# First tiles by half products, up behind three runs, and VectorE's order within a step

## The reference, cut to what matters

```python
y    = conv1d(x, weight, groups=4, pad=4) + (c @ c_weight.T)[:, :, None] + bias[None, :, None]
base = y @ base_W.T + base_b                          # 512 -> 512
p    = softmax(y @ router_W.T + router_b)             # 15 routes
w    = sum of the top 8 p, by expert (expert_map)     # 8 experts
h    = y @ A.T                                        # 8 experts x rank 16
out  = x + base + 2 * ((h * w) @ B.T)
```

## Time and profile before

| what | value |
|---|---|
| median of three runs | 184.21 us (184.16 to 184.89) |
| the profiled execution's own time | 184.34 us |
| its span in the trace | 182.5 us |
| TensorE busy | 178.0 us, 98% of the span |
| VectorE busy | 151.0 us, 83% |
| GpSimd busy | 139.7 us, 77% |
| ScalarE busy | 81.6 us, 45% |
| chain that ended last | TensorE 92%, DMA 5%, VectorE 1% |

### The profile page before, as it was taken

The page is one execution under the profiler, slowest core; times in us unless marked ns, Lnnn a source line. Parts: engine busy times, 40 slices in busy tenths (PEclk is TensorE's granted clock), DMA queues, the critical chain, the costliest instruction groups (busy, mean ns, idle before and its releaser), DMA issues.

```text
span 182.5 us, 3929 instructions
## 1 busy us (share of the span) xinstructions
PE 178.0 (98%) x1236; PEld 170.9 (94%) x1236; DVE 151.0 (83%) x510; ACT 81.6 (45%) x247; POOL 139.7 (77%) x138
## 2 busy tenths in 40 slices
PE   7999999999999999999999999999999999999993
PEld 3777999999999999999999999999999999999992
DVE  0597888898898889888888988889898888978673
ACT  3568743354544434454433445444344545422320
POOL 2118999999888898888889888888988888885610
PEclk9999999999999999999999999999999999999999
DMA  6999951767475654637475454756536721233304
GB/s 160 355 347 288 340 190 11 234 193 213 161 231 176 187 169 123 198 131 230 132 232 164 133 166 163 230 178 196 188 101 160 278 83 61 94 115 115 119 0 172
DMA packets 17876, 32.01 MB, mean 175 GB/s; under 512 B 1984, under 2 KB 3136, under 8 KB 17856
## 3 DMA queue, kind: packets, MB, share of 16 engines
q1 hardware_dynamic: 17424, 31.40, 53.7%
q10 hardware_dynamic: 432, 0.36, 0.6%
HBM read 23.36 MB, written 8.39 MB: 174 GB/s over the span
## 4 chain that ended last, share of the span: by engine, by line
PE 92%; DMA 5%; DVE 1%; ACT 0%; SPq 0%; issue 0%; DVEq 0%
PE wide_ps L604 61%; PE wide_ps L646 12%; PE conv_banks L590 11%; DMA wide_sb<-wide_w 3%; PE edge_bank L590 3%; PE conv_banks L604 2%; PE odd_bank L633 2%; DMA x_in<-x_first 2%; PE conv_banks L563 1%; PE conv_banks L561 1%; DVE xr L979 1%; ACT wide_hi L356 0%; SPq L257 0%; PE conv_banks L646 0%; PE edge_bank L633 0%
## 5 line engine op out<-in xcount | busy, mean ns | idle before, releaser
L604 PE MATMUL wide_ps<-wide_hi,y_hi 128*128 128x400 f32 (+1 forms) x248 | 66.1, 326 | 0.3 <-ACT wide_hi L356 0.3
L604 PE MATMUL wide_ps<-wide_hi,y_lo 128*128 128x400 f32 (+1 forms) x248 | 62.6, 312 | 0.0
L604 PE MATMUL wide_ps<-wide_lo,y_hi 128*128 128x400 f32 (+1 forms) x248 | 62.4, 312 | 0.0
L484 POOL TENSOR_TENSOR terms_lo<-terms,terms_hi 128x512 fp32r<-128x512 f32 x28 | 36.3, 1297 | 18.2 <-ACT terms_hi L385 18.2
L604 PEld LDWEIGHTS wide_ps<-wide_hi,y_hi 128*128 128x128 f32 x248 | 44.0, 188 | 2.5 <-ACT wide_hi L356 0.6
L604 PEld LDWEIGHTS wide_ps<-wide_lo,y_hi 128*128 128x128 f32 x248 | 45.9, 188 | 0.0
L604 PEld LDWEIGHTS wide_ps<-wide_hi,y_lo 128*128 128x128 f32 x248 | 45.8, 188 | 0.0
L502 POOL TENSOR_TENSOR y_lo<-y,y_hi 128x512 fp32r<-128x512 f32 x31 | 40.3, 1298 | 5.0 <-ACT y_hi L400 5.0
L479 POOL TENSOR_TENSOR xr<-xr,base_b_sb 128x512 f32<-128x512 f32 x32 | 41.7, 1302 | 0.0
L407 ACT ACTIVATE hw_hi<-odd_bank 128x128 fp32r<-128x128 f32 x31 | 8.6, 278 | 54.3 <-PE odd_bank L633 54.3
L779 DVE TENSOR_TENSOR xr<-wide_ps,xr 128x512 f32<-128x512 f32 x30 | 20.7, 691 | 5.3 <-PE wide_ps L646 4.0
(11 more groups left out here) (90 smaller groups left out, 308.8 us busy)
## 6 DMA issues: line engine op xcount, KB each, us to landing
xr<-x_rows SPq DMA_DIRECT2D x32, 256.0 KB, 3.6
out<-xr SPq DMA_DIRECT2D x31, 256.0 KB, 3.3
terms<-x_units SPq DMA_DIRECT2D x28, 256.0 KB, 2.8
edges<-x_edges SPq DMA_DIRECT2D x14, 256.0 KB, 3.2
wide_sb<-wide_w SPq DMA_DIRECT2D x4, 328.0 KB, 5.0
x_in<-x_first SPq DMA_DIRECT2D x3, 264.0 KB, 5.3
weights_sb<-conv_w SPq DMA_DIRECT2D x2, 192.0 KB, 5.8
x_in<-x_first SPq DMA_DIRECT2D x2, 132.0 KB, 2.8
```

Source lines behind the costliest of these rows:

```text
L484: nc.gpsimd.tensor_tensor(terms_lo[i % 2][:, :, :, :], terms[i][:, :, :, :], terms_hi[i % 2][:, :, :, :].bitcast(F32), ALU.subtract)\
L604: mm = nc.tensor.matmul(sums_of(t, k)[:, b, 0:columns[1] - columns[0]], a[k % 2][:, r, :], w[:, r, columns[0]:columns[1]], start=r == 0 an ...
```

## The change

Tiles 2 and 3 no longer come as plain blocks: they are loaded as pairs of terms, as the later tiles are, and `conv_whole` makes them with float32 products of 256 columns: the odd terms by summed weights, the difference by own weights, and, for tile 2 alone, the edges of both tiles. The differences of these tiles are made by GpSimd (tile 2 and the edges) and VectorE (tile 3). In step 0 a `W_REST` run stands ahead of HIGH of run 2. The loads at the start have a new order and new waits, and `base_b` comes as 128 full rows. The bias of the first four tiles is added by GpSimd after the output sum (`bias_sums`) and no longer before it. SyncE issues the load of the next rows ahead of the store. `up` stands behind three runs from step 2 on (two in step 1, three before). The edges of tiles 4 and 6 are made within steps 2 and 4, ahead of `up`. On VectorE `condition` is cut in two (`condition` and `reach`); from step 6 on a step is: condition, hw_low, choose, best, reach, mark, difference, add_out, weigh, turn. Steps 2 to 5 have orders of their own. ScalarE makes `y_high` right behind `hw_high` (behind the exponentials in steps 2 to 4). The last two steps are as before.

The core of the diff:

```diff
+            def conv_whole(t):
+                i, h = t - FIRST, t % 2
+                pe.wait_ge(y_rows_ready, t - 1)
+                pe.wait_ge(conv_w_in[2 + i], 16)
+                pe.wait_ge(first_terms_in[i], 16)
+                nc.tensor.matmul(conv_ps[:, h, 0, :, :], conv_sb[:, W_SUM[t], :],
+                                 first_terms[i][:, 1, :, :], start=True, stop=True)
+                pe.wait_ge(first_difference[i], 1)
+                mm = nc.tensor.matmul(conv_ps[:, h, 1, :, :], conv_sb[:, W_OWN[t], :],
+                                      first_terms[i][:, 0, :, :], start=True, stop=True)
+                if h == 0:
+                    pe.wait_ge(cond_biased, GROUPS)
+                    pe.wait_ge(first_edge_ready, 1)
+                    mm = nc.tensor.matmul(edge_ps, conv_sb[:, W_QUARTERS[t // 2], :],
+                                          first_edges[:, 0, :, :], start=True, stop=True)
+                mm.then_inc(conv_done, 1)
...
                 y_rest(0)
                 y_rest(1)
+                w_rest(0)
                 high(2)
                 y_rest(2)
-                w_rest(0)
+                w_rest(1)
...
             def second_step():
                 linear(1, 1, runs, (FRONT_BANK,), (W_REST,))
+                conv_whole(3)
                 pe.wait_ge(y_lo_ready, 2)
                 linear(1, 1, runs, (FRONT_BANK,), (Y_REST,)).then_inc(front_done, 1)
-                conv_later(3)
                 turn_hw(0, 0)
-                linear(1, 1, runs[:3], (NEXT_BANK,))
+                linear(1, 1, runs[:2], (NEXT_BANK,))
                 up(0, 0)
-                linear(1, 1, runs[3:], (NEXT_BANK,)).then_inc(linear_done, 1)
+                linear(1, 1, runs[2:], (NEXT_BANK,)).then_inc(linear_done, 1)
+                conv_blocks(START, 0)
...
                     turn_hw(t - 1, k - 1)
-                    linear(t, k, runs[:2], (NEXT_BANK,))
+                    linear(t, k, runs[:3], (NEXT_BANK,))
+                    if t == 2 or t == 4:
+                        conv_edges(t + 2, (k + 2) % GROUPS, p + 1).then_inc(conv_done, 1)
                     up(t - 1, k - 1)
-                    linear(t, k, runs[2:], (NEXT_BANK,)).then_inc(linear_done, 1)
+                    linear(t, k, runs[3:], (NEXT_BANK,)).then_inc(linear_done, 1)
...
+                if up_to_tile(t, 5):
+                    if t == 5:
+                        turn(t + 1, k + 1)
+                    hw_low(t - 1, k - 1)
+                    choose(t, k)
+                    dve.wait_ge(logits_ready, t + 1)
+                    best(t, k)
+                    if t < 5:
+                        turn(t + 1, k + 1)
+                    else:
+                        condition(t + 2, (k + 2) % GROUPS, q + (k + 2) // GROUPS)
+                        reach(t + 2, (k + 2) % GROUPS)
+                    dve.wait_ge(top_ready, t + 1)
+                    mark(t, k)
+                    difference(t + 4, k)
+                    add_out(t - 1, (k - 1) % UNROLL)
+                    weigh(t, k)
...
+                best(t, k)
+                if up_to_tile(t, TILES - 5):
+                    reach(t + 2, (k + 2) % GROUPS)
...
+                dve.wait_ge(top_ready, t + 1)
+                mark(t, k)
+                if up_to_tile(t, TILES - 5):
+                    difference(t + 4, k)
+                if up_to_tile(t, TILES - 3):
+                    add_out(t - 1, (k - 1) % UNROLL)
+                weigh(t, k)
+                if up_to_tile(t, TILES - 5):
+                    turn(t + 2, k + 2)
```

The loads at the start, in SyncE's order, and ScalarE's order ahead of step 1:

```diff
             load_conv(2)
-            load_x(2)
-            sync.wait_ge(wide_in[0], 16)
+            load_first_terms(0)
+            sync.wait_ge(wide_in[1], 16)
+            sync.dma_start(first_edges[:, :, :, :], x_edges[0]).then_inc(first_edges_in, 16)
+            load_conv(4)
+            sync.wait_ge(wide_in[2], 16)
             load_conv(3)
-            load_x(3)
-            sync.wait_ge(wide_in[2], 16)
+            load_first_terms(1)
+            sync.wait_ge(wide_in[3], 16)
             load_terms(START, 0)
             load_edges(START // 2, 0)
             sync.dma_start(up_sb[:, :], up_w).then_inc(up_in, 16)
...
             y_high(1, 1, 2)
+            exponentials(0, 0)
             odd_up(START, 0)
-            exponentials(0, 0)
-            terms_high(START, 0)
             act.wait_ge(up_in, 16)
             nc.scalar.activation(up_hi[:, :], up_sb[:, :], ACT.Copy, scale=LORA_SCALE)\
                 .then_inc(up_hi_ready, 1)
             nc.scalar.activation(up_scaled[:, :], up_sb[:, :], ACT.Copy, scale=LORA_SCALE)\
                 .then_inc(up_scaled_ready, 1)
+            terms_high(START, 0)
             edge_high(START // 2, 0)
```

More of the change, by code:

```diff
@@ L519, in step @@
                 if t == 0:
+                    up_low()
                     terms_low(t + 4, k)
-                    up_low()
                     edge_low(p + 2, k // 2)
+                    y_low(t + 2, k + 2)
                     pool.wait_ge(base_b_in, 16)
-                    bias_rows(t, k)
-                    y_low(t + 2, k + 2)
+                    bias_sums(0)
                     return
@@ L544, in step @@
                         edge(p + 3, 1 - k // 2)
+                if from_tile(t, 3) and up_to_tile(t, POST + 1):
+                    bias_sums(t - 2)
             steps_of(step)
@@ L565, in conv_first, with products, conv_blocks @@
                     .then_inc(conv_done, 1)
-            def conv(t, g, p):
+            def products(sums, j, hi, lo):
+                for w, a in ((conv_hi, hi), (conv_lo, hi), (conv_hi, lo)):
+                    mm = nc.tensor.matmul(sums, w[:, j, :], a[:, :, :],
+                                          start=w is conv_hi and a is hi, stop=a is lo)
+                return mm
+            def conv_blocks(t, g):
                 h = g % 2
                 pe.wait_ge(terms_lo_ready, t - START + 1)
[L571 to L583, removed]
+                pe.wait_ge(y_rows_ready, t - 1)
@@ L584, in conv @@
                 if t < 2 * START and h == 0:
                     pe.wait_ge(conv_lo_ready, 2 + g // 2 * 2)
[L586 to L589, removed]
-                        mm = nc.tensor.matmul(sums, w[:, j, :], a[:, :, :],
-                                              start=w is conv_hi and a is hi, stop=a is lo)
+                products(conv_ps[:, h, 0, :, :], S_SUM[g], terms_hi[h][:, 1], terms_lo[h][:, 1])
@@ L641, in up @@
                     for a, w in ((hw_hi, up_hi), (hw_hi, up_lo), (hw_lo, up_hi)):
+                        if w is up_lo and not from_tile(t, 1):
+                            pe.wait_ge(up_lo_ready, 1)
                         if a is hw_lo and n == 0:
@@ L922, in step @@
                 if t == 0:
-                    condition_first(2)
+                    condition(2, 2, 0)
+                    hw_low(0, 0)
+                    reach(2, 2)
                     turn(2, 2)
@@ L927, in step @@
                     best(1, 1)
+                    return
+                if t == 1:
+                    add_out(0, 0)
                     dve.wait_ge(top_ready, 2)
                     mark(1, 1)
-                    condition_first(3)
-                    hw_low(0, 0)
+                    difference(START + 1, 1)
+                    weigh(1, 1)
+                    condition(3, 3, 0)
+                    reach(3, 3)
                     return
-                if t == 1:
-                    turn(3, 3)
-                    difference(START + 1, 1)
-                    add_out(0, 0)
-                    weigh(1, 1)
+                if up_to_tile(t, 5):
[7 more added lines that the diff above has]
+                        turn(t + 1, k + 1)
+                    else:
+                        condition(t + 2, (k + 2) % GROUPS, q + (k + 2) // GROUPS)
[5 more added lines that the diff above has]
+                    weigh(t, k)
+                    if t < 5:
+                        condition(t + 2, (k + 2) % GROUPS, q + (k + 2) // GROUPS)
+                        reach(t + 2, (k + 2) % GROUPS)
+                    else:
+                        turn(t + 2, k + 2)
                     return
@@ L940, in step @@
                     condition(t + 2, (k + 2) % GROUPS, q + (k + 2) // GROUPS)
+                if from_tile(t, TILES - 4) and up_to_tile(t, TILES - 3):
+                    reach(t + 2, (k + 2) % GROUPS)
+                if t == TILES - 3:
                     turn(t + 2, k + 2)
-                    hw_low(t - 1, k - 1)
-                elif t == TILES - 2:
+                if up_to_tile(t, TILES - 2):
                     hw_low(t - 1, k - 1)
```

156 lines of the change are left out of this document (101 added, 55 removed).

## The result

The changed kernel takes 188.95 us, the median of five runs (188.63 to 189.22); a sixth run, at 990.07 us, was a slow one and is left out. The kernel before, beside it, takes 184.70 (six runs, 184.16 to 184.91). The ratio is 1.0227, interval 1.0198 to 1.0257. The change is slower, as forecast, but by 4.25 us where 1.4 was forecast, and 188.95 lies outside the range of 183.4 to 186.8. The profiled execution took 189.22, its span is 187.4; before, 184.34 and 182.5, so there are 4.9 us to find.

What follows compares the result with a forecast made beforehand. TensorE, 98% busy, was taken as the bound, with VectorE's chain at nearly the same period. 0.50 us lost by step 6 plus 0.90 in even steps gave 1.40 on 184.34: 185.74, as median 185.6; range 183.4 to 186.8.

Steps and rivals of the forecast that it cites:

- product count: TensorE at the start: tiles 2 and 3 take five products of 0.43, 2.15 us against 3.44, 1.29 less.
- tile 3: TensorE at the start: tile 3's two products of 256 columns take 0.86 us.
- late up weights: Start: 304 KB more ahead of the up weights, 0.7 us taken; `up` of tile 0 at 18.7, 0.6 late.
- Steps 2 to 5: Other orders there lose 0.08 us each in steps 2 and 4, 0.20 in 3, 0.46 in 5.
- The even steps: Even steps 6 to 28, without edges: the output sum waits for `up`; 0.075 us lost each, 0.90 in all.
- the price of `up` by itself: `up` behind three runs: output sum starts at 4.375 after the front, next front at 5.205 where 5.13 was due.
- The sign: Whole kernel: the change makes it slower, by 0.8%; slower (above 185.1) had chance 0.52.
- The first (wait just met): Even steps: nothing lost, only the 0.50 us of the first steps is left; 184.7 us. Chance 0.20.
- the second (TensorE dense): All steps: output sums come in time everywhere, TensorE stays dense; 182.6 us, faster. Chance 0.12.
- the third (up weights on time): Start: up weights land as early as before, first steps end 0.7 us earlier; 184.9 us. Chance 0.13.
- The fourth: Start: VectorE's tile 3 difference and GpSimd's instruction exclude each other, 1.4 us; 185.3 with early up weights. Chance 0.05.
- The fifth: Both upper ends: up weights 0.9 late, 0.125 per even step, sum 0.05 late on VectorE; 187.0 us. Chance 0.08.

Runs made afterwards that it cites:

- both moves undone: The changed kernel with `reach` straight behind `condition` and `up` behind two runs, both from step 6 on: 185.81 us, ratio 1.0077 to the kernel before.

## Why the prediction was wrong

**The product count and tile 3 were right.** In the kernel with both moves undone tile 3's two products take 0.87 (from 15.89, four products of 0.73 behind the start of a run at 15.16, to 16.76, the same ahead of the transpose at 17.49); 0.86 was said.

**The late up weights were right, where the start was early enough to show them.** The kernel with both moves undone, timelines of ScalarE, TensorE, VectorE and GpSimd, for the earlier trace rows:

```profile
16.55 0.63 ACT L443 ACTIVATE up_hi<-up_sb 128x512 fp32r<-128x512 f32 x1 [1.03 <-DMA up_sb<-up_w]
...
18.44 0.25 ACT L427 ACTIVATE hw_hi<-odd_bank 128x128 fp32r<-128x128 f32 x1
```
```profile
18.84 0.47 PE L700 MATMUL wide_ps<-up_hi,hw_hi 128*128 128x256 f32 x2 [0.37 <-ACT hw_hi L427]
```
```profile
14.29 0.51 DVE L997 TENSOR_TENSOR first_terms<-first_terms 128x256 f32<-128x256 f32 x1 [0.19 <-DMA first_terms<-x_units]
```
```profile
14.48 1.48 POOL L532 TENSOR_TENSOR y_lo<-y,y_hi 128x512 fp32r<-128x512 f32 x1
```

`up_hi` starts at 16.55 (16.38 said), `hw_hi` at 18.44 (18.30), `up` at 18.84 (18.7), step 2 at 21.39 (21.15). In the changed kernel's own profile step 2 starts at 21.81, for two reasons no step named. The first products took longer (last section), so that `up` was not late there. And the front of step 2 waits 0.3 for the sum of tile 0, behind `reach` of tile 2 on the upper partitions: from the front of step 1 it takes 6.34, and 6.05 in the kernel with `reach` on partitions 0 to 63, whose first products were late too.

**Steps 2 to 5.** Said 5.56, 5.33, 5.56 and 5.94, measured 5.57, 5.27, 5.57 and 6.13. The mechanism is the one given; step 5 was too short by 0.19. VectorE in step 5 of the changed kernel:

```profile
41.31 0.29 DVE L955 TENSOR_TENSOR hw_lo<-odd_bank,hw_hi 128x128 fp32r<-128x128 f32 x1
...
41.81 0.41 DVE L872 TENSOR_TENSOR y_rows<-conv_banks,cond_sb 128x256 f32<-128x256 f32 x1
42.25 0.42 DVE L876 TENSOR_TENSOR y_rows<-conv_banks,y_rows 128x256 f32<-128x256 f32 x1
42.71 0.42 DVE L887 TENSOR_TENSOR y_rows<-edge_bank,y_rows 64x256 f32<-64x256 f32 x1
...
43.52 0.68 DVE L853 TENSOR_TENSOR xr<-wide_ps,xr 128x512 f32<-128x512 f32 x1
```

From `hw_low` to the sum 2.21, said 2.24; but `hw_low` has no wait in front of it and starts 3.09 behind the front (38.22), not 2.87. VectorE was already behind. The reader is to see the missing bracket. With `reach` on partitions 0 to 63 step 5 takes 5.97, so that most of the 0.19 has the cause of the next paragraph.

**The even steps: here the prediction failed.** Its step was "So 4.2 to 4.5; the wait for `up` decides, or is missed by 0.1 at most". The place is right, the price of `up` by itself is right (5.205 said, 5.20 to 5.23 in three kernels), and yet the wait for `up` doesn't decide: VectorE is ready at 4.56, 0.19 past it, in ten of eleven steps (in step 8 the sum starts at 4.71, for another, open reason). Against the profiled execution the sum was short by 3.5 us (4.9 - 1.4): 2.35 in these eleven steps (3.17, where 11 x 0.075 = 0.82 was said), 0.66 for the start of step 2, 0.15 for steps 2 to 5 and 0.34 for the odd steps. The durations from `hw_low` to the sum had been added to 1.63 (it is 1.69), 4.5 behind the front, and I took less, since a follower can start before the printed end of the instruction ahead of it. The earlier trace rows held both kinds of pair: the match starts 0.02 ahead of the output sum's printed end, but the transpose behind `reach` starts 0.46 after it, past its printed 0.43. I took the first kind for all of them, and `reach` is the instruction that the change moved into the chain. Behind the sum, load and product cost 0.16 where I took 0.14. The sign was not luck: with VectorE's lateness taken away and `up` left where the change puts it, the kernel still takes 186.77, more than the kernel before.

The Trainium skill has a rule that gives this (VectorE: DVE Perf Modes, section "Two Vector instructions with no wait between them"): an instruction whose inputs or output start in another quadrant of partitions than the last read or write in that memory is held until every earlier Vector instruction has finished. The trace agrees for `reach`, the match and the difference behind it in even steps, 0.11 + 0.14 + 0.13 late, and none of it when `reach` stays on the lower partitions. The prediction didn't weigh this rule; it spoke against the change.

**Rivals.** The first (wait just met) and the second (TensorE dense) fall by the 13 waits. Of the third (up weights on time) only this is seen: `up` is not late in executions whose start is late, and that saves nothing there. The fourth, that VectorE's difference and GpSimd's `y_lo` exclude each other, holds in its form, and its price was hidden, as said. In the rows above VectorE's difference starts first, and `y_lo` takes 1.48 where it takes 1.30 on average. In the kernel with the move of `up` alone undone `y_lo` starts first (timelines of GpSimd and VectorE):

```profile
14.42 1.29 POOL L532 TENSOR_TENSOR y_lo<-y,y_hi 128x512 fp32r<-128x512 f32 x1
```
```profile
14.45 1.55 DVE L997 TENSOR_TENSOR first_terms<-first_terms 128x256 f32<-128x256 f32 x1 [0.41 <-DMA first_terms<-x_units]
```

Now the difference takes 1.55 instead of some 0.4 and ends 0.29 behind the end of `y_lo`. In the changed kernel it starts at 15.05 while GpSimd's `conv_lo` runs (14.70 to 15.57), takes 0.80 and ends 0.28 behind that. In both it ends only behind GpSimd's instruction, as the rival had it (spans of GpSimd are rough). With late up weights this costs nothing: step 2 starts at 21.41 where the difference took 1.55, at 21.39 where it took 0.51. The Trainium skill (SBUF — State Buffer, section "Who interferes with whom") says that such instructions contend; the trace agrees, with 1.1 us on the difference in the rows just shown. The fifth had the right sign in its second part: it priced VectorE's lateness at 0.05 in each even step, and it was 0.19.

**What stays open.** In the kernels with `up` behind two runs, step 25 takes 5.77 to 5.79: ScalarE's `hw_hi` starts 0.28 later behind its transpose than elsewhere (it does so too where `up` stands behind three runs, and is hidden there). The kernel before has no such step. In step 8 of the kernels made from the changed one the sum starts 0.87 to 0.89 behind `up`'s last pair, where elsewhere 0.5 is enough (except with `up` alone undone, where VectorE's chain ends later); in the kernel before it doesn't, with `up` behind two runs or three. Nothing in the profile names what holds either. Odd steps lose up to 0.06 each in the changed kernel; this wasn't traced. And of 1.6 us that TensorE was spared at the start at most some tenths are seen in any start of step 2 (21.02 to 21.81 against 21.79, with 0.35 of edge products moved behind it); which wait each tenth went to was followed only for `up` and for the sum of tile 0.

## What to carry to other kernels

Two engines with nearly equal periods make each other's limit: before an instruction is moved ahead of the one that releases the other engine, lay its chain out start to start, and take the overlap of neighbours only for a pair that a row shows overlapping. An instruction on another range of partitions costs its neighbours more than its own row says; keep it where the engine waits anyway (here behind `condition`, ahead of the wait for `hw_hi`). Where a start has two conditions, lift each alone and both together: undoing `up` alone showed nothing here, and yet it is worth 0.07 a step once the other is lifted.

## What was not expected of the hardware

The half of the partitions that a small VectorE instruction works on changes its own start and those of the match and the difference behind it, by 0.11 to 0.14 us each. In the step ahead of step 2 the same shows as 0.3 us (6.34 against 6.05).

The first float32 products behind the bf16 ones on zeros take different times in different executions, at the full granted clock in the page's row in both. TensorE's timeline of the changed kernel, and of the kernel before:

```profile
3.64 2.93 PE L715 MATMUL conv_banks<-x_in,weights_sb 128*128 128x256 f32 x6
```
```profile
3.68 1.94 PE L661 MATMUL conv_banks<-x_in,weights_sb 128*128 128x256 f32 x6
```

The same six took 2.06 us from 3.74 in the kernel with both moves undone. Over the nine traces they take 1.94 to 2.28 in six and 2.88 to 2.93 in three. Everything behind them moves: ScalarE's `y_hi` of tile 1 starts at 14.68 against 13.46 and 13.64. Over the nine traces it lies between 13.46 and 14.68. This explains most of the change's late step 2 (the front of step 1 starts at 15.47, and at 14.43 with both moves undone), and why starts from a single profile can't be compared to better than a us; what makes these products slow was not tried.
